# Self-attention of three transformer layers: P is normalised by a product with a diagonal, not by scaling its rows

## The reference

```python
scores = jnp.einsum('bihd,bjhd->bhij', q, k) * scale      # 512 x 512 for each of 4 x 16 pairs of batch and head
p = jax.nn.softmax(scores, axis=-1)
out = jnp.einsum('bhij,bjhd->bihd', p, v)
```

## Time and profile before

| | us |
|---|---|
| runs of the kernel before (3) | 5093.52, 5093.72, 5094.57; median 5093.72 |
| the profiled execution: its own time | 5091.53 |
| the profiled execution: span from first to last instruction | 5089.6 |
| TensorE busy in that span | 4705.9 |
| VectorE, ScalarE, GpSimd busy | 3726.7, 2257.5, 2708.1 |
| mean granted clock of TensorE | 0.971 of full speed |

### The profile page before, as it was taken

How to read it: one execution, slowest core, us unless ns; L and a number is a source line. 1 busy time by engine, 2 the same in 40 slices (tenths; PEclk the granted TensorE clock), 3 DMA queues, 4 the chain that set the end, 5 groups by cost and what they waited for, 6 DMA issues and landing times.

```text
span 5089.6 us, 53152 instructions
## 1 busy us (share of the span) xinstructions
PE 4705.9 (92%) x18768; PEld 2603.1 (51%) x18768; DVE 3726.7 (73%) x3613; ACT 2257.5 (44%) x3966; POOL 2708.1 (53%) x1431
## 2 busy tenths in 40 slices
PE   7888899898988888878999899999999999999999
PEld 4555555555555555434555544555554445555544
DVE  4999999999999999886777625666654256665531
ACT  5556555555556555534444434334333233334331
POOL 2666666666666666556888215666521056665210
PEclk9999999999999999998999999999999999999999
DMA  3444444444444444430000100000101000001000
GB/s 117 152 155 153 158 142 158 152 155 156 154 153 158 153 156 151 144 111 7 1 1 13 40 19 1 1 1 1 46 5 42 0 1 1 1 1 50 1 1 17
DMA packets 110962, 372.64 MB, mean 73 GB/s; under 512 B 28016, under 2 KB 32880, under 8 KB 107760
## 3 DMA queue, kind: packets, MB, share of 16 engines
q1 hardware_dynamic: 110704, 369.26, 20.6%
HBM read 365.94 MB, written 3.28 MB: 73 GB/s over the span
## 4 chain that ended last, share of the span: by engine, by line
PE 49%; DVE 3%; ACT 1%; POOL 1%; issue 1%; DVEq 0%; ACTq 0%; POOLq 0%
PE PS L1160 7%; PE PS L1170 6%; PE PS L1185 6%; PE PS L1139 5%; PE PS L1349 5%; PE PS L1360 3%; PE PS L1148 3%; PE PS L1196 2%; PE PS L1309 2%; PE PS L1270 2%; PE PS L1279 1%; PE PS L1296 1%; PE PS L1288 1%; PE PS L1126 1%; ACT PA L1434 1%
## 5 line engine op out<-in xcount | busy, mean ns | idle before, releaser
L635 POOL TENSOR_TENSOR UH<-UH,BC 128x1152 f32<-128x1152 f32 x512 | 1344.2, 2625 | 920.0 <-DVE U L683 920.0
L1101 POOL TENSOR_SCALAR PA<-PA,INV 128x512 f32<-128x512 f32 x768 | 1189.6, 1569 | 551.6 <-DVE INV L1621 551.6
L691 DVE TENSOR_TENSOR_SCAN UH<-DA,U 128x1152 f32<-128x1152 f32 x512 | 1307.2, 2553 | 24.4 <-ACT DA L575 7.0
L384 PE MATMUL Y<-UH,ident_sb 128*128 128x512 f32 (+1 forms) x3072 | 1117.5, 508 | 201.7 <-DVE ZS L698 104.8
L384 PEld LDWEIGHTS Y<-UH,ident_sb 128*128 128x128 f32 x3072 | 568.0, 196 | 788.4 <-issue 539.4
L1434 ACT ACTIVATE PA<-PS,NMX 128x512 f32<-128x512 f32 x768 | 519.4, 684 | 720.5 <-DVE NMX L1615 566.3
L575 ACT ACTIVATE DA<-DT,NEGA 128x575 f32<-128x575 f32 x1024 | 718.9, 763 | 101.3 <-DVE UH L691 67.3
L683 DVE TENSOR_TENSOR U<-DTX,BC 128x1152 f32<-128x1152 f32 x512 | 698.9, 1365 | 56.5 <-DMA BC<-bc_rows 10.1
L1630 DVE COPY VP<-PS 128x512 f32<-128x512 f32 x768 | 495.2, 686 | 256.9 <-PE PS L1170 235.2
L1615 DVE TENSOR_REDUCE NMX<-PS 128x2 f32<-128x1024 f32 x384 | 452.5, 1219 | 58.4 <-PE PS L1160 58.4
L1170 PEld LDWEIGHTS PS<-ident_sb,PA 128*128 128x128 f32 x3072 | 351.8, 142 | 241.4 <-issue 193.5
(11 more groups left out here) (153 smaller groups left out, 4929.6 us busy)
## 6 DMA issues: line engine op xcount, KB each, us to landing
BC<-bc_rows SPq DMA_DIRECT2D x512, 576.0 KB, 3.7
ARENA<-mamba_a SPq DMA_DIRECT2D x16, 1421.0 KB, 7.4
ARENA<-pair_w SPq DMA_DIRECT2D x4, 3072.0 KB, 10.3
WB<-mamba_b SPq DMA_DIRECT2D x16, 514.0 KB, 5.0
VP<-ff_w SPq DMA_DIRECT2D x2, 3072.0 KB
WO<-out_w SPq DMA_DIRECT2D x4, 1024.0 KB
stream<-x_t SPq DMA_DIRECT2D x2, 1024.0 KB, 9.9
ARENA<-pair_w SPq DMA_DIRECT2D x4, 512.0 KB, 5.5
```

The lines of the kernel that those rows point to most:

```text
L384: mm = pe.matmul(Y[:, a:b], IDENT[:, :], UH[:, SLOT[j], a:b], start=(s == 0), stop=(s == DS - 1), skip_group_check=True)
L635: pool.tensor_tensor(h, h, BC[:, j % NBB, 1, :].unsqueeze(1).broadcast_to([P, HK, T]), ALU.mult).then_inc(s_hc, 1)
L691: dve.tensor_tensor_scan(UH[:, SLOT[j], :], DA[:, j % NDA, :], U[:, 0:HC], 0.0, ALU.mult, ALU.add).then_inc(s_scan, 1)
L1101: pool.tensor_scalar(PR[:, n % 3, j, :], PR[:, n % 3, j, :], INV[:, n % 4, j:j + 1], None, ALU.mult).then_inc(s_ps, 1)
```

## The change

The inverse sums no longer scale the rows of P. GpSimd multiplies the identity matrix by them instead, which gives a 128 x 128 diagonal matrix for each head of each step. TensorE then turns a piece of P by an ordinary matmul with that diagonal where it had a transpose with the identity: with the piece of P as weights W, the product W^T x diag(r) is the transpose of diag(r) x W. `DIAG` has three buffers, so GpSimd now waits until step `ng-3` was turned. The order of all engines' instructions and the other waits are as they were.

```diff
+        DIAG = sb("DIAG", [P, 3, 2, P])
...
                         pool.wait_ge(s_r, START + ng + 1)
+                        pool.wait_ge(s_tp, START + 2 * (ng - 2) if ng >= 3 else START)
                         for j in range(2):
-                            pool.tensor_scalar(PR[:, n % 3, j, :], PR[:, n % 3, j, :], INV[:, n % 4, j:j + 1], None,
+                            pool.tensor_scalar(DIAG[:, ng % 3, j, :], IDENT[:, :], INV[:, n % 4, j:j + 1], None,
                                                ALU.mult).then_inc(s_ps, 1)
...
                             for kt in range(QT):
-                                mm = pe.transpose(PS[:, B_T + j, kt * P:(kt + 1) * P], PR[:, n % 3, j, kt * P:(kt + 1) * P],
-                                                  IDENT[:, :])
+                                mm = pe.matmul(PS[:, B_T + j, kt * P:(kt + 1) * P], PR[:, n % 3, j, kt * P:(kt + 1) * P],
+                                               DIAG[:, ng % 3, j, :], start=True, stop=True)
                             mm.then_inc(s_tp, 1)
```

More of the change, by code:

```diff
@@ L967, in transformer_layers @@
         s_r = step("t_inverse")
-        s_ps = step("t_probs_scaled")
+        s_ps = step("t_inverse_diagonals")
         s_tp = step("t_probs_turned")
```

## The result

The changed kernel takes 5402.48 us in the median of four runs (5400.94 to 5405.35), the kernel before 5094.15 us beside it. The ratio is 1.0606, with a 95% interval of 1.0588 to 1.0624: slower by 308 us. Forecast were 5412 us, with a range of 5372 to 5455.

The account below looks back on a forecast made before the run. TensorE's own work was taken to bound self-attention. Span 5089.6 + 349.4 for the turn - 31 for returned stalls and clock = 5408.0; 5409.9 as execution time, 5412 us with 2.2 to the median; range 5372 to 5455.

Parts of the forecast that it names:

- The turn: Line 1170 on TensorE: two records per piece, 0.87 to 1.78 us a turn, +349.4 us over 384 steps.
- rival 3: Turn on TensorE: weight loads not hidden, 390 ns a piece, +863 us, 5957 us; chance 0.02.
- rival 4: Turn on TensorE: a piece costs four times a transpose, +1005 us, 6098 us; chance 0.01.
- The return: Layer 0's self-attention: stalls and slow clock give back 31 us; nothing taken in layers 1 and 2.
- 5.4 + 12: TensorE's idle time in layer 0: 5.4 us back from three 2.7 us stalls, some 12 from other waits.
- level: Layer 0 before the change: two steps take TensorE 5.6 us and VectorE 5.5 us.
- Rival 1: Layer 0: layer norms still delay the copies, stalls stay and the clock falls, 5443 us; chance 0.09.
- the 0.2 us: GpSimd's scaling in layer 0: taking work off it is worth at most TensorE's one wait, 0.2 us.
- that port: GpSimd's port on SBUF: used less, which can only help VectorE's layer-norm operations; no size given.
- The diagonal's cost: GpSimd's new 128 x 128 operation, line 1101: some 0.45 us each, 768 of them, beside TensorE's work.
- no waits for GpSimd: Sign expected in the profile after: TensorE never waits for GpSimd.
- The added wait: GpSimd's wait until step `ng-3` was turned: already met when the inverse sums arrive, cost 0.

Follow-up runs that it names:

- e2: Kernel before with the transposes replaced by ordinary matmuls with the identity, GpSimd scaling P as before: 5406.38 us, ratio 1.0616.
- e6: Changed kernel with P and the diagonals held and multiplied as float32r, P in a tensor of its own: 5087.02 us, ratio 0.9984.
- e4: Kernel before with the last step of self-attention's layer norm on VectorE done in two parts, one step pair apart: 5071.34 us, ratio 0.9955.
- e5: Changed kernel with the last step of the layer norm done in two parts: 5399.72 us.
- e1: Changed kernel with the transposes put back; GpSimd still builds the diagonals, P is not normalised: 5085.93 us, ratio 0.9986.
- e7: Changed kernel with float32r products with the diagonal and the layer norm in two parts: 5084.07 us, ratio 0.9973.
- e9: Kernel before with the layer norm in two parts and float32r products with a rounded identity for transposes: 5091.04 us, ratio 0.9996.
- e8: Changed kernel with transposes put back, P not normalised, and the layer norm in two parts: 5075.17 us, ratio 0.9965.

## Why the prediction was right

**The turn.** The term that decided was read from its neighbour: 0.89 us for eight records of line 1279, and so 1.78 us for a turn. The chain after shows 1.78 us, and 6144 records. e2 and e6 fix it from both sides: full 32-bit matmuls instead of transposes bring the loss without any diagonal, and a product with the diagonal in one record does not bring it. The loads of weights, 192 ns each, stayed hidden, which puts rival 3 out; rival 4's factor of four does not appear in any run: 1.78 against 0.87 us is 2.05.

**The return.** 31 us were forecast in layer 0 and nothing in the others. Layer 0 gave back 116.5 - 83 = 33 us: 17 of idle time, 13.6 of slow clock (half of 27.2), and some 2 between records. The parts came out as forecast too: 17.2 us of idle time for 5.4 + 12, though of the three long waits nothing stayed where I had let 0.9 us of each stay. Layers 1 and 2 gave 3 and 4 us, of which 2.2 and 2.7 are idle time, where I had taken none; their growth of 113 instead of 116 is the term that was a little off.

Beyond the forecast the three layers gave back some 10 us in all (2, 3 and 4). That is the size of the miss, 5412 to 5402, but not its whole account. In the profiled executions the span was to be 5408.0 us and is 5403.6: the three layers took 10 us less than forecast, and 5.6 us more were spent ahead of layer 0. The other 5 us of the miss are scatter: the median lies 2.9 us below the profiled execution after the change, where it lay 2.2 us above it before.

The argument for the return used a sum that was off: the 5.6 us of TensorE, "level" with VectorE's 5.5, had the turn of layer 1. Layer 0's own chain, before and then after, has

```profile
2446.89 1.92 PE PS L1160 x8
2448.80 1.02 PE PS L1170 x8
2449.82 1.85 PE PS L1185 x16
2451.68 1.19 PE PS L1170 x8
```

```profile
2442.43 1.98 PE PS L1172 x16
2444.41 1.85 PE PS L1187 x16
2446.26 1.98 PE PS L1172 x16
2448.24 1.92 PE PS L1162 x8
```

which is 6.0 us for two steps before and 7.7 after. VectorE had 0.5 us to spare in two steps already, too little to make good a block of 3.2 us in time; with 2.2 us it could. The turns here grew by 0.96 and 0.79 us instead of 0.91 twice, so a few of the 33 us may be work that was never added. Rival 1, stalls that stay, is out. Its mechanism was the right one to ask for: e4 shows that the norm's block makes the stalls, and e5 that the change leaves nearly none.

**GpSimd.** Here a step of the prediction failed, though it cost nothing. I took the 0.2 us that TensorE waited for GpSimd as all that GpSimd was worth. e1 gained 8 us with GpSimd's part alone, most likely because its long operations also lengthen VectorE's norm from 2.5 to 3.3 us, and the wait then stands under VectorE's name. On top of TensorE's part it is worth 4 us (e2 against the change). I had named that port as something that can only help and given it no number. The diagonal's cost was 605 ns and not 450: a quarter of the elements took 39% of the time. And I expected no waits for GpSimd; there were six, 3.9 us in all.

**The added wait** for step `ng-3` does not appear among what GpSimd waited for after the change: VectorE's inverse ended 1578.6 of its 1579.0 us of idle time. The 5 us that I gave a step are 3.7 us in layer 0 before and 4.4 after (the stage over 128 steps), still far more than the 1.2 us of two diagonals.

## What to carry to other kernels

Before a transpose is made to do a second job as a matmul, count the records that an ordinary matmul of that type leaves against the instructions issued: the mean duration hides a factor of two. Work taken off an engine that is not the fullest is worth only the stalls that it causes, also those that stand under another engine's name, and a saving there that adds to the fullest engine is paid in full. In an in-order queue that runs nearly level with its consumer, one long block is worth cutting in two: here it gave 23 us, where the change cost 308.

## What was not expected of the hardware

- A float32r matmul of 128 x 128 by 128 columns took one record of 105 ns (0.84 us for eight), less than a 32-bit transpose at 109 ns; a full 32-bit one took two of 111 ns.
- With the norm in two parts, TensorE's clock stood at 0.96 over layer 0 past its first 25 us with float32r products (e7, e9) and at 1.00 with transposes (e4, e8). Gaps of 0.67 to 0.82 us came ahead of the low stretches of e7, while gaps of 1.0 us in e4 had none behind them.
- VectorE's norm operations on SBUF took up to 1181 and 904 ns beside GpSimd's 1569 ns operations, and 742 to 747 and 480 to 482 ns in e1, where none of them ran beside one; its copies out of PSUM stayed at 685 to 690 ns.
